# Arrival counts and the dense-tile list move into the last three turns' Vector code; the f2 broadcast moves to the dense block

## The reference, cut to what matters

```
h = max(layernorm(x), 0)
f1 = h @ a[:256];  f2 = h @ a[256:]
e = leaky_relu(f1 + f2.T, 0.2)
U = softmax(where(adj > 0, e, -9e15), axis=1)
rowsum = sum(U * 0.5 U, axis=1)
feat = soft_threshold(mix(U @ h, h * rowsum, h))      # first propagation
pu = U @ feat                                         # second propagation
out = x + mix(feat, pu, rowsum, h0)
```

## Time and profile before

| what | value |
|---|---|
| median of 3 runs | 1465.8 us (1458.76 to 1468.39) |
| profiled execution, its own time | 1463.31 us |
| its span, first to last instruction | 1461.7 us |
| mean granted clock of TensorE | 0.821 |
| DVE busy | 958.1 us (66%) |
| ACT busy | 854.0 us (58%) |
| PE busy | 907.1 us (62%) |
| POOL busy | 590.2 us (40%) |
| end of DVE's tail in block one | about 1076.7 us |
| first DVE instruction of block three | 1079.76 us |

### The profile page before, as it was taken

One profiled execution on the slowest core, in us unless ns is written; L12 is line 12 of the kernel. 1 busy time (PEld: TensorE's weight loads), 2 busy tenths in 40 slices (PEclk: granted clock), 3 DMA queues, 4 the chain that ended last, 5 costly groups with the idle time before them and its releaser, 6 DMA issues. The chain is left out here.

```text
span 1461.7 us, 27565 instructions
## 1 busy us (share of the span) xinstructions
PE 907.1 (62%) x3386; PEld 532.5 (36%) x3449; DVE 958.1 (66%) x5343; ACT 854.0 (58%) x1817; POOL 590.2 (40%) x645
## 2 busy tenths in 40 slices
PE   0015776667767667776776776776625574666666
PEld 0001244344444333433333333443414453544434
DVE  5877646777887888888887878887750122333453
ACT  3274387678888888888888888887321212121111
POOL 2003405444433333232212212221227777777775
PEclk9975588989998998989777777777657877888998
DMA  4979688789999999999999999997234556677886
GB/s 95 338 263 320 226 359 299 294 334 388 396 369 375 379 373 386 376 384 376 365 372 361 350 377 358 357 367 292 65 113 121 164 161 195 201 216 225 242 258 202
DMA packets 151066, 427.17 MB, mean 292 GB/s; under 512 B 30123, under 2 KB 112697, under 8 KB 134516
## 3 DMA queue, kind: packets, MB, share of 16 engines
q1 hardware_dynamic: 120872, 348.93, 64.3%
q0 software_dynamic: 30160, 77.90, 17.5%
HBM read 401.29 MB, written 33.85 MB: 298 GB/s over the span
## 5 line engine op out<-in xcount | busy, mean ns | idle before, releaser
L297 ACT ACTIVATE SG<-W,ABOVE 128x4096 bf16<-128x4096 f32 x126 | 467.0, 3706 | 59.3 <-DVE cnt L904 55.1
L585 POOL DMA_INDIRECT R<-haug_d,IDS x228 | 230.2, 1009 | 624.5 <-issue 624.5
L309 PE MATMUL TP<-SG,FOLD 128*128 128x512 bf16 x1006 | 307.0, 448 | 67.9 <-ACT SG L297 63.6
L627 ACT ACTIVATE DG<-ident,WSR 128x128 f32<-128x128 f32 x228 | 75.0, 391 | 314.3 <-PE ACC L641 292.0
L1515 DVE SCALAR_TENSOR_TENSOR W<-ACC,SELF,W 128x256 f32<-128x256 f32 x63 | 30.5, 484 | 243.7 <-PE ACC L641 243.7
L636 PE MATMUL ACC<-R,DG 128*128 128x256 f32 x538 | 183.6, 489 | 0.0
L309 PEld LDWEIGHTS TP<-SG,FOLD 128*128 128x128 bf16 x1008 | 114.9, 123 | 181.7 <-ACT SG L297 64.8
L635 PE MATMUL ACC<-XHO,ZB 128*128 128x256 bf16 x127 | 39.8, 314 | 209.4 <-DMA R<-feat_d,IDT 75.5
L636 PEld LDWEIGHTS ACC<-R,DG 128*128 128x128 f32 x538 | 120.4, 240 | 20.1 <-issue 0.3
L585 POOL DMA_INDIRECT R<-feat_d,IDR x115 | 110.3, 959 | 35.1 <-issue 33.2
L585 POOL DMA_INDIRECT W<-feat_d,IDR x113 | 108.6, 961 | 34.4 <-issue 33.5
(11 more groups left out here) (273 smaller groups left out, 2169.8 us busy)
## 6 DMA issues: line engine op xcount, KB each, us to landing
W<-in_adj_dram SPq DMA_DIRECT2D x128, 2048.0 KB, 10.3
haug_d<-R POOLq DMA_DIRECT2D x8, 1056.0 KB, 8.0
HTS<-haug_d SPq DMA_DIRECT2D x64, 132.0 KB
R<-in_x_dram SPq DMA_DIRECT2D x8, 1024.0 KB, 6.3
feat_d<-FTS SPq DMA_DIRECT2D x64, 128.0 KB, 1.7
W<-in_x_dram SPq DMA_DIRECT2D x64, 128.0 KB
W<-in_L_gnn_h_dram SPq DMA_DIRECT2D x64, 128.0 KB
W<-feat_d SPq DMA_DIRECT2D x64, 128.0 KB
```

Of the source, the lines that this page charges most:

```text
L297: nc.scalar.activation(SG[:, u, half(h)], W2[:, u, half(h)], ACT.Sign, scale=2.0 ** 100, bias=ABOVE[:], accum_out=DEG[:, u, h:h + 1]).then ...
L309: nc.tensor.matmul(KP[u], FOLD[:, b], SG[:, u, b * FW:(b + 1) * FW], start=False, stop=False)
L585: pool.indirect_dma_start(out=g[:, k, 0:w], out_offset=None, in_=table, in_offset=bass.IndirectOffsetOnAxis(ap=ids[:, k:k + 1], axis=0), * ...
L627: nc.scalar.mul(DG[:, u, k], ident[:], weights[:, k:k + 1])
```

## The change

Three edits.

The tail's operations on `lkey`, `ARR`, `COUNT` and `LIST` leave the tail and become 18 groups. A new call `aside(t, i)`, at eight places in DVE's turn, issues one group each in the turns 63, 64 and 65. The running count is now made by doubling (offsets 4, 8, 16, 32), so five steps stand where 15 additions stood, four of them with a copy beside the addition. Turn 63 holds the six arrival groups and the two flag groups, turn 64 the eight pairs of L1111 and L1112, and turn 65 the last two operations.

The place of the asides: 0 after L918, before the wait for `MOV`; 1 after L923; 2 after L931; 3 after L940; 4 after L947; 5 after L957; 6 after L960; 7 after L966.

The broadcast of f2 leaves SP's turn 61 and goes into block two's loop over dense tiles, and the waits for it go from the head of block two into that loop.

```diff
@@ -647,7 +647,2 @@
                 def body(t, q, u, live):
-                    if isinstance(t, int) and t == NS - 2:
-                        for h in range(2):
-                            sp.wait_ge(sg_ready[1][h], NS // 2)
-                        sp.wait_ge(f2_stored, 16)
-                        sp.dma_start(F2B, f2_d.rearrange("t p -> (t p)").rearrange("(one n) -> one n", one=1).broadcast_to([P, N])).then_inc(f2b_loaded, 16)
                     if live(2):
@@ -885,2 +880,52 @@
 
+                L_ = Steps(dve, s1_step, NS * 29 + 4 * HEAD, 10 + 2 * (NT // 8))
+
+                def arrivals(i):
+                    if i == 0:
+                        L_.mark(ts(lkey[:, 0], CTL[:, :, 0], 16.0, None, ALU.mult))
+                    elif i <= 4:
+                        w, a_, b_ = RING << (i - 1), 1 - i % 2, i % 2
+                        L_.need()
+                        nc.vector.tensor_copy(lkey[:, b_, 0:w], lkey[:, a_, 0:w])
+                        L_.mark(tt(lkey[:, b_, w:], lkey[:, a_, w:], lkey[:, a_, 0:NT - w], ALU.add))
+                    else:
+                        L_.need()
+                        L_.mark(nc.vector.tensor_copy(ARR[:], lkey[:, 0]))
+
+                def flagged(i):
+                    if i == 0:
+                        L_.need()
+                        L_.mark(stt(lkey[:, 0], FLG[:], 0.0, ONE_R[:], ALU.is_gt, ALU.mult, accum_out=ksm[:, 3:4]))
+                    else:
+                        L_.need()
+                        nc.vector.tensor_copy(COUNT[:], ksm[:, 3:4])
+                        L_.mark(tt(lkey[:, 1], lkey[:, 0], back[:], ALU.mult))
+
+                def pick(i):
+                    a_, b_ = 1 - i % 2, i % 2
+                    L_.need()
+                    L_.mark(mx(lkey[:, 2, 8 * i:8 * i + 8], lkey[:, a_]))
+                    L_.need()
+                    L_.mark(swap(lkey[:, b_], lkey[:, 2, 8 * i:8 * i + 8], lkey[:, a_], 0.0))
+
+                def listed(i):
+                    if i == 0:
+                        L_.need()
+                        L_.mark(ts(lkey[:, 0], lkey[:, 2], -1.0, float(NT), ALU.mult, ALU.add))
+                    else:
+                        L_.need()
+                        L_.mark(ts(LIST[:], lkey[:, 0], float(NT - 1), None, ALU.min))
+
+                def aside(t, i):
+                    if isinstance(t, int) and t >= NS:
+                        i += 8 * (t - NS)
+                        if i < 6:
+                            arrivals(i)
+                        elif i < 8:
+                            flagged(i - 6)
+                        elif i < 16:
+                            pick(i - 8)
+                        elif i < 18:
+                            listed(i - 16)
+
                 def body(t, q, u, live):
@@ -918,2 +963,3 @@
                         ts(SCR[:, ub, K:K + 1], SSELF[:, cb], 0.0, None, ALU.add)
+                    aside(t, 0)
                     if on:
@@ -923,2 +969,3 @@
                         B_.mark(ts(scr, MOV[:, 0:K], F1[:, cb], None, ALU.add))
+                    aside(t, 1)
                     if on:
@@ -931,2 +978,3 @@
                         B_.mark(stt(scr, scr, ALPHA, scr, ALU.mult, ALU.max))
+                    aside(t, 2)
                     if on:
@@ -940,2 +988,3 @@
                         B_.mark(tt(scr, scr, PENM[:, ub], ALU.min))
+                    aside(t, 3)
                     if on:
@@ -947,2 +996,3 @@
                         B_.mark(nc.vector.reduce_max(m[:, 0:1], SCR[:, ub], AX.X))
+                    aside(t, 4)
                     if on_c:
@@ -957,2 +1007,3 @@
                         nc.vector.tensor_scalar_mul(m[:, 1:2], m[:, 0:1], -1.0).then_inc(top_ready, 1)
+                    aside(t, 5)
                     if on_c:
@@ -960,2 +1011,3 @@
                         C_.mark(stt(q_z, s[:, 3:4], invz, invz, ALU.mult, ALU.mult))
+                    aside(t, 6)
                     if on:
@@ -966,2 +1018,3 @@
                         C_.mark(stt(coef, q_z, -0.5, one_m[:, 2:3], ALU.mult, ALU.add))
+                    aside(t, 7)
                     if on:
@@ -1086,5 +1139,6 @@
                     body(t, t // 2, t % 2, lambda l: 0 <= t - l < NS)
-
-
-                step = Steps(dve, s3_step, NS * 7, 11 + 2 * (NT // 8) + NT // RING)
+                L_.end()
+
+
+                step = Steps(dve, s3_step, NS * 7, 9)
                 dve.wait_ge(lists_kept, NS)
@@ -1093,4 +1147,3 @@
                 step(nc.vector.reduce_sum(ZQ[:, 0, 1:2], QB0[:], AX.X))
-                nc.vector.reciprocal(INVZ[:], ZQ[:, :, 0])
-                step(ts(lkey[:, 1], CTL[:, :, 0], 16.0, None, ALU.mult))
+                step(nc.vector.reciprocal(INVZ[:], ZQ[:, :, 0]))
                 step(tt(ROWS[:], ZQ[:, :, 1], INVZ[:], ALU.mult))
@@ -1101,15 +1154,2 @@
                 feat_steps(step, ACC0, HT0, INVZ[:, 0:1], ROWS[:, 0:1], M0[:, 0:1], T0[:], FTS[:, 1]).then_inc(feat0_made, 1)
-                for r in range(1, NT // RING):
-                    step(tt(lkey[:, 1, RING * r:RING * r + RING], lkey[:, 1, RING * r:RING * r + RING],
-                            lkey[:, 1, RING * (r - 1):RING * r], ALU.add))
-                nc.vector.tensor_copy(ARR[:], lkey[:, 1])
-                step(stt(lkey[:, 0], FLG[:], 0.0, ONE_R[:], ALU.is_gt, ALU.mult, accum_out=ksm[:, 3:4]))
-                nc.vector.tensor_copy(COUNT[:], ksm[:, 3:4])
-                step(tt(lkey[:, 1], lkey[:, 0], back[:], ALU.mult))
-                for i in range(NT // 8):
-                    a_, b_ = 1 - i % 2, i % 2
-                    step(mx(lkey[:, 2, 8 * i:8 * i + 8], lkey[:, a_]))
-                    step(swap(lkey[:, b_], lkey[:, 2, 8 * i:8 * i + 8], lkey[:, a_], 0.0))
-                step(ts(lkey[:, 0], lkey[:, 2], -1.0, float(NT), ALU.mult, ALU.add))
-                ts(LIST[:], lkey[:, 0], float(NT - 1), None, ALU.min)
                 step.end()
@@ -1183,2 +1223,3 @@
                     sp.wait_ge(a_free, n + 1)
+                    sp.dma_start(F2B, f2_d.rearrange("t p -> (t p)").rearrange("(one n) -> one n", one=1).broadcast_to([P, N])).then_inc(f2b_loaded, 16)
                     for c in range(2 * CP):
@@ -1195,3 +1236,2 @@
             def _(act):
-                act.wait_ge(f2b_loaded, 16)
                 act.sem_inc(a_free, 1)
@@ -1225,3 +1265,2 @@
             def _(dve):
-                dve.wait_ge(f2b_loaded, 16)
                 for u in range(2):
@@ -1238,2 +1277,3 @@
                             cc = n * CP + c2
+                            dve.wait_ge(f2b_loaded, 16 * n + 16)
                             dve.wait_ge(sgn_ready, 2 * cc + u + 1)
```

## The result

The changed kernel takes 1457.45 us (median of 20 runs, 1452.55 to 1466.84) against 1460.74 us for the kernel before in the same measurement (20 runs, 1456.96 to 1468.39). The ratio is 0.9971 with a 95% interval of 0.9959 to 0.9983, so about 4.2 us faster, with 2.5 to 6.0 covered. It is a small gain, real by the interval and well within 1%. The profiled execution took 1457.48 us, its span is 1455.8 us.

A forecast was written before the change was run, and what follows sets the result against it. Block three's start was taken to set the end, with SP waiting 6.4 us for DVE's lists at block one's end. 6.4 - 1.9 = 4.5 us off the median 1465.8 gave 1461.3 us, range 1454.5 to 1467.5.

The forecast's parts named there:

- The gain's ceiling, 6.4 us: End of block one: taking the lists out of the tail gains at most SP's wait there, 6.4 us.
- Turn 63, 0.3 us: L923 to L957 in turn 63: four copies and four additions delay it by 0.3 us, bounds 0 and 1.2.
- Turn 64 before L957, 1.4 us: L923 to L957 in turn 64: four dependent pairs delay it by 1.4 us, bounds 1.3 and 2.24.
- Behind L957, 0.2 us: L957 of turn 64 to the last L997: three pairs and two list operations make DVE outlast PE by 0.2 us.
- The shift of `feat0_made`, 1.9 us: End of block one: the moved list work makes `feat0_made` later by 0.3 + 1.4 + 0.2 = 1.9 us.
- The sum, 4.5 us: Whole kernel: SP's wait of 6.4 us less the delay of 1.9 us gives 4.5 us less.
- The broadcast, 0 us: Turn 60: moving the 4096 KB broadcast gains 0 us, as no wait is put down to a DMA; bounds 0 and 3.2.
- Rival A: Turns 63 and 64: fillers cost their full durations, shift 3.9 us, 2.5 us gained, 1463.3 us; chance 0.17.
- Rival B: Turn 60: the broadcast did hold it up, 3.2 us more gained, 7.7 in all, 1458.1 us; chance 0.08.
- Rival C: DVE's queue: every aside's wait holds it and pauses cover nothing; 1.2 us slower, 1467.0 us; chance 0.06.
- Rival D: Anywhere: something the rows don't show, such as the code's new layout, either way, no size given; chance 0.06.

The follow-up runs named there:

- Experiment 5: Changed kernel with turn 63 as it was, but the eight pairs and last two list operations behind `feat0_made`; ratio 0.9966 to the kernel before.
- Experiment 6: Changed kernel with turn 64's four pairs from before L957 moved behind it, seven pairs there in all; ratio 0.9970 to the kernel before.
- Experiment 4: Changed kernel with the same 18 groups placed where DVE pauses, some behind `feat0_made`; ratio 0.9963 to the kernel before, 0.9950 on chip 4.
- experiment 3: Kernel before with the 4096 KB broadcast of f2 sent a second time, in SP's turn 62; ratio 1.0026 to the kernel before.
- experiments 1 and 2: 1: changed kernel with the broadcast back in its old place, 0.9968, again 0.9977. 2: kernel before with only the broadcast moved, 0.9991, again 1.0011.

## Why the prediction was right

**The gain's ceiling, 6.4 us: right.** SP's wait is 0.2 us, the end of block one is SP's. Experiment 5 shows the other side: with the pairs left in the tail, DVE is last and SP waits again.

**Turn 63, 0.3 us: 0.42 measured.** Eight fillers whose durations sum to 1.46 us cost 1.35 - 0.93. At L923 of turn 64 this arrives in full in three traces (changed, and the lists alone twice), by half in the changed kernel on chip 4 (21.21), and not at all in experiments 5 and 6, by way of PE's clock. No step had that.

**Turn 64 before L957, 1.4 us: 1.42 measured** (2.34 - 0.92), against 2.24 for four pairs at full length. Experiment 4 removes it and L923 to L957 is short again.

**Behind L957, 0.2 us: nothing.** From L957 to the last L997 it is 1065.65 - 1060.48 = 5.17 us, 5.19 before. DVE was ready at 1065.51, 5.03 us behind L957: at the low end of the 5.0 to 5.7 that the prediction gave, so PE still led, by a tenth. For the three pairs the prediction has "by the same allowance 1.2 at least"; in proportion (1.3 of 2.24, times 1.7) it would be 1.0 us. Nothing hangs on it. Experiment 6 shows how near the edge is: four more pairs cost 2.3 us there.

**The shift of `feat0_made`, 1.9 us: 1.79.** From it to block three 11.7 us became 5.45, where 5.3 was forecast. The sum, 4.5 us, stands beside 4.47 in the trace and 4.2 (2.5 to 6.0) in the runs. That it agrees to the tenth is in part luck: the terms of turn 63 and behind L957 miss by 0.1 and 0.2 us and partly cancel, the ceiling was 6.3 (11.71 - 5.45) and not 6.4, and the clock alone moves the distance by up to 0.4 us from one execution to the next. The predicted 1461.3 us was made on the median shown then, 1465.8; in the measurement of the result the kernel before stands at 1460.74, and the changed one at 1457.45. The distance of 3.9 us to the prediction is mostly the scatter of medians (the kernel before alone moved by 5.1), not a step of the sum. Nor does the time say much by itself: the range of 13 us would have held the kernel before as well. What bears the prediction out is the sequence of waits in the trace.

**The broadcast, 0 us: right where measured alone, for a reason that was incomplete.** The prediction argued that no wait is put down to a DMA, and so there is nothing to gain. On chips 1 and 2 nothing was gained, and in the changed kernel the stall of 2.9 us in turn 60 is still there. What it did not ask is how much later the gathers could land before DVE notices. They share the DMA engines with 4096 KB for 13.3 us and DVE asks for them 1 us after that the earlier trace rows. What the gathers lose by it, some 7 us of a margin of 9, and what is left show in experiment 3.

**Rival A** (full durations) falls with turn 63 and turn 64: 0.42 and 1.42 us where it had 1.2 and 2.24. The score operation that follows a filler starts 0.13 us behind an addition of 0.20 us. The Trainium skill's rule in "VectorE: DVE Perf Modes", The DRAIN you can't avoid, which the prediction named for this rival, has an exception in the same place, which the prediction left out: "A next op that is not held starts earlier". The trace agrees with the exception. **Rival B**, 3.2 us from turn 60, falls with experiments 1 and 2 on chips 1 and 2, and holds in a small form, one trace, on chip 4. **Rival C** falls: the pauses did cover what was put into them. **Rival D** has nothing to show; the code's new layout left the other stages as they were, within their scatter. One part of the change has no run of its own: the doubling, which makes five steps of 15 additions. What it would gain in the tail by itself isn't measured.

## What to carry to other kernels

Before moving work off the end of a stage, read how long the other engines stood waiting there: that wait, not the length of the work, is the ceiling. Then put the work where the receiving engine pauses, not merely between its operations: 18 small groups interleaved cost 1.8 us of a gain of 6.3, and put into the pauses 0.2. "No wait is put down to this transfer" says that it is free now. How free it is, the distance says between the landing of what shares the DMA engines with it and the next use of that.

## What the runs showed of the hardware

Small DVE operations on one partition cost by their place: between two dependent operations of 0.17 us a copy and an addition together cost 0.1 us (0.42 / 4), a dependent pair of L1111 and L1112 0.36 us (1.42 / 4) of its 0.56.

A delay of PE by 0.4 us was taken back in two of six traces with fillers between L923 and L957 of turn 63, and by half in a third. There the granted clock went from 0.50 to 1.00 earlier relative to the work, by a microsecond between the changed kernel and experiment 5; L827 then takes 0.30 us instead of 0.46. It isn't the fillers that do it: the kernel with two broadcasts, which has none, gets the same, and in the first trace of the kernel before the clock stays at 0.50 through the whole of turn 64. What made it rise earlier, the traces don't show.

A transfer of 4096 KB in flight for 13.3 us holds up the small gathers that are issued within 3 us of its start: their last packet ends some 7 us later than without it.

Chips differ: the same kernel before takes 1463.95 us on one and 1611.41 us on another, and the traced kernels have 379 to 382 us for block three on the one and 477 to 483 on the other, with nearly equal distances from turn 62 to it.
